# A flamingo-style stack of eight blocks: the second half of a mixture's gathers and additions moved into the attention behind it

## What is computed

```python
# layer 0, feed-forward (router on the normalised x)
topv, topi = jax.lax.top_k(probs, 2)
topv = topv / (topv.sum(axis=-1, keepdims=True) + 1e-09)
h = gelu(einsum('td,edh->teh', xf, w1)); y = einsum('teh,ehd->ted', h, w2)
out = einsum('te,ted->td', cw, y)
# layer 1, cross-attention (X: normalised x, C: context)
sim = sigmoid(sim_beta + sim_alpha * einsum('bkd,btd->bkt', C, X))
mask = one_hot(argmax(sim, axis=1), K, axis=1)
agg = einsum('bkt,btd->bkd', sim * mask, X) + C
out_k = agg / (sum(mask, axis=-1, keepdims=True) + 1.0)
out = X + einsum('bkt,bkd->btd', sim, out_k)
# in both cases
x = x + tanh(gate) * out
```

## Time and profile before

| what | value |
|---|---|
| median of 3 runs | 1840.54 us (1837.99 to 1843.1) |
| the profiled execution | 1836.82 us |
| its span, first to last instruction | 1835.1 us |
| granted PE clock over the span | 0.917 |
| PE, DVE, ACT, POOL busy | 1515.9, 1082.8, 683.5, 782.4 us |
| last experts' matmul to the attention's first instruction | 509 to 559.7 us |
| competitive attention | 559.7 to 642.9 us |

### The profile page before, as it was taken

The page is one execution under the profiler, slowest core; times in us unless marked ns, Lnnn a source line. Parts: engine busy times, 40 slices in busy tenths (PEclk is TensorE's granted clock), DMA queues, the critical chain, the costliest instruction groups (busy, mean ns, idle before and its releaser), DMA issues. The chain is left out here.

```text
span 1835.1 us, 32265 instructions
## 1 busy us (share of the span) xinstructions
PE 1515.9 (83%) x10543; PEld 1188.7 (65%) x10543; DVE 1082.8 (59%) x2434; ACT 683.5 (37%) x1673; POOL 782.4 (43%) x1037
## 2 busy tenths in 40 slices
PE   2998786799905786888887888789999999869997
PEld 1776675699904654666664444578778788658874
DVE  2666763323436978677775888455465765444555
ACT  2555443233304332344443333244454544411121
POOL 1444374513362444344443333145445377533335
PEclk9999897899955588899998999899999999969999
DMA  8000003477610000000000000000000000048853
GB/s 276 28 0 2 1 26 108 142 224 234 191 51 4 0 1 1 1 0 0 0 0 1 0 0 0 1 1 0 0 1 1 1 17 15 25 126 238 234 160 87
DMA packets 90876, 100.94 MB, mean 55 GB/s; under 512 B 11156, under 2 KB 73804, under 8 KB 90125
## 3 DMA queue, kind: packets, MB, share of 16 engines
q1 hardware_dynamic: 53490, 69.07, 12.2%
q0 software_dynamic: 8192, 16.79, 3.2%
q10 hardware_dynamic: 29083, 13.66, 2.6%
HBM read 70.92 MB, written 28.57 MB: 54 GB/s over the span
## 5 line engine op out<-in xcount | busy, mean ns | idle before, releaser
L427 POOL TENSOR_TENSOR exp_scores<-exp_scores,softmax_recip 128x308 f32<-128x308 f32 x256 | 181.7, 742 | 242.8 <-DVE softmax_recip L590 242.7
L916 POOL DMA_INDIRECT gathered_rows_ffn<-sorted_y,slot_ffn x128 | 121.0, 945 | 212.5 <-DMA sorted_y<-expert_rows_ffn 143.0
L612 PE MATMUL psum<-identity,exp_scores 128*77 128x128 f32 x1024 | 157.0, 290 | 41.1 <-POOL exp_scores L427 37.9
L1115 PE MATMUL psum<-sorted_transposed_ffn,tile_weights_ffn 128*128 128x256 f32 x736 | 184.2, 394 | 2.5 <-DVE sorted_transposed_ffn L1023 2.4
L612 PEld LDWEIGHTS psum<-identity,exp_scores 128*77 128x77 f32 x1024 | 119.6, 154 | 66.6 <-issue 32.6
L1773 POOL TENSOR_TENSOR exp_scores_xattn<-exp_scores_xattn,softmax_recip_xattn 128x1640 f32<-128x1640 f32 x32 | 93.5, 2921 | 160.8 <-DVE softmax_recip_xattn L1946 160.8
L442 ACT COPY probs_transposed<-psum 77x512 f32<-77x512 f32 x192 | 111.8, 584 | 131.8 <-PE psum L612 130.3
L1115 PEld LDWEIGHTS psum<-sorted_transposed_ffn,tile_weights_ffn 128*128 128x128 f32 x736 | 135.8, 195 | 27.6 <-DVE sorted_transposed_ffn L1023 12.2
L1124 PE MATMUL psum<-tile_weights_ffn,hidden_ffn 128*128 128x128 f32 x1104 | 138.5, 276 | 0.0
L700 PE MATMUL psum<-probs_transposed,v_padded 77*32 77x128 f32 x2048 | 128.9, 275 | 6.7 <-ACT probs_transposed L442 6.7
L1124 PEld LDWEIGHTS psum<-tile_weights_ffn,hidden_ffn 128*128 128x128 f32 x1104 | 131.0, 192 | 0.2
(11 more groups left out here) (358 smaller groups left out, 3402.8 us busy)
## 6 DMA issues: line engine op xcount, KB each, us to landing
tile_weights_ffn<-in_L_ffn_packed_dram SPq DMA_DIRECT2D x46, 512.0 KB, 3.5
tile_weights_ffn<-in_L_ffn_packed_dram SPq DMA_DIRECT2D x46, 384.0 KB, 3.4
sorted_rows_ffn<-sorted_x SPq DMA_DIRECT2D x92, 128.0 KB, 3.9
sorted_y<-expert_rows_ffn ACTq DMA_DIRECT2D x92, 128.0 KB, 3.3
sorted_x<-zeros SPq DMA_DIRECT2D x4, 1472.0 KB, 13.7
x_residual<-in_x_dram SPq DMA_DIRECT2D x4, 512.0 KB, 11.6
sorted_x<-xn_ffn,slot_ffn POOLq DMA_INDIRECT x128, 2.2
gathered_rows_ffn<-sorted_y,slot_ffn POOLq DMA_INDIRECT x128, 3.0
```

The costliest lines, as they stand in the source:

```text
L427: nc.gpsimd.tensor_tensor(e[:, par, heads, :], e[:, par, heads, :], rec.to_broadcast([S, HG, KC]), ALU.mult).then_inc(s["probs_ready"], 1)
L612: last = nc.tensor.transpose(m.psum[0:KC, 4 + g % 2, h * S:(h + 1) * S], e[:, nxt, g * HG + h, :], m.ident[:, :])
L916: nc.gpsimd.indirect_dma_start(yg[:, n % 4, k, :], None, m.sorted_y[half][:, :], bass.IndirectOffsetOnAxis(slot[:, half, k, b:b + 1], 0)). ...
L1115: mm = nc.tensor.matmul(m.psum[:, 2 * (n % 2) + half, c * TILE:(c + 1) * TILE], w[:, n % DEPTH, at:at + 128], xst[:, n % 2, :], start=True ...
```

## The change

The mixture of layer 0 is built with `tail=False`: POOL gathers nothing for the last 16 batches, and DVE's last loop of additions is gone. Both are now in the competitive attention, which takes the routing `r` (slots, weights and the gather buffers, that moved to it).

- POOL issues the gathers of four batches before step 0 and of three behind its own work of each of steps 0 to 3.
- DVE adds four batches at the end of step 0 and three at the end of each of steps 1 to 4, first all first rows, then all second rows, then the statistics.
- The attention's first variance, square root and reciprocal are of the first 16 batches. Those of batches 16 to 23 are taken between steps 2 and 3 and those of batches 24 to 31 between steps 4 and 5: DVE's five instructions at the end of a step, ACT's square root and the table of the exponential again at the start of the next, DVE's reciprocal and shift ahead of its next step.
- All ten steps are written out; the loop is gone (`looped=2`).

```diff
+        self.gathered = sb("gathered_rows", [S, 4, 2, D])
...
-                    for b in range(HBATCH):
+                    for b in range(HBATCH if tail or half < HALVES - 1 else 0):
...
-                else:
+                elif tail:
                     for n in range(B - HBATCH, B):
                         combine(n)
...
+    FIRST = 4
+    PER_STEP = 3
+    MIDDLE = B - HBATCH + HBATCH // 2
+    STATS = {2: (B - HBATCH, MIDDLE, 1), 4: (MIDDLE, B, 2)}
+
+    def late_of(g):
+
+        if g < 0:
+            return range(0, FIRST)
+        return range(min(FIRST + g * PER_STEP, HBATCH), min(FIRST + (g + 1) * PER_STEP, HBATCH))
...
+                def gather(g):
+                    for i in late_of(g):
+                        n = B - HBATCH + i
+                        wait(pool, s["late_combined"], i - 3)
+                        for k in range(2):
+                            nc.gpsimd.indirect_dma_start(r.gathered[:, n % 4, k, :], None, m.sorted_y[HALVES - 1][:, :],
+                                                         bass.IndirectOffsetOnAxis(r.slot[:, HALVES - 1, k, i:i + 1], 0)).then_inc(m.gathered[0][n % 4], 16)
...
                 def step(g, par, front, middle, back):
+                    if g < 0:
+                        gather(g)
                     if middle:
...
+                    if g >= 0:
+                        gather(g)
+
+                pipeline(pool, step, NGB, looped=2)
...
-                nc.scalar.activation(m.sd[:, :], m.var[:, :], ACT.Sqrt, bias=m.eps[:, 0:1]).then_inc(s["sd_ready"], 1)
+                first = slice(0, B - HBATCH)
+                nc.scalar.activation(m.sd[:, first], m.var[:, first], ACT.Sqrt, bias=m.eps[:, 0:1]).then_inc(s["sd_ready"], 1)
...
+                    if g - 1 in STATS:
+                        lo, hi, before = STATS[g - 1]
+                        act.wait_ge(s["var_ready"], before + 1)
+                        nc.scalar.activation(m.sd[:, lo:hi], m.var[:, lo:hi], ACT.Sqrt, bias=m.eps[:, 0:1]).then_inc(s["sd_ready"], 1)
+                        preload(nc, m, ACT.Exp)
+                        act.wait_ge(s["shift_ready"], before + 1)
...
-                variance_of_x(nc, m, dve, s["parts_ready"], s["var_ready"])
-                rstd_of_x(nc, m, dve, s["sd_ready"], s["rstd_ready"], s["shift_ready"])
+                variance_of_x(nc, m, dve, s["parts_ready"], s["var_ready"], 0, B - HBATCH)
+                rstd_of_x(nc, m, dve, s["sd_ready"], s["rstd_ready"], s["shift_ready"], 0, B - HBATCH)
...
+                def combine(g):
+                    late = late_of(g - 1)
+                    for i in late:
+                        n = B - HBATCH + i
+                        dve.wait_ge(m.gathered[0][n % 4], 32 * (n // 4 + 1))
+                        nc.vector.scalar_tensor_tensor(m.x[:, n, :], r.gathered[:, n % 4, 0, :], r.weight[:, HALVES - 1, 0, i:i + 1], m.x[:, n, :],
+                                                       ALU.mult, ALU.add).then_inc(s["late_first"], 1)
+                    for i in late:
+                        n = B - HBATCH + i
+                        dve.wait_ge(s["late_first"], i + 1)
+                        nc.vector.scalar_tensor_tensor(m.x[:, n, :], r.gathered[:, n % 4, 1, :], r.weight[:, HALVES - 1, 1, i:i + 1], m.x[:, n, :],
+                                                       ALU.mult, ALU.add).then_inc(s["late_combined"], 1)
+                    for i in late:
+                        n = B - HBATCH + i
+                        dve.wait_ge(s["late_combined"], i + 1)
+                        nc.vector.bn_stats(m.moments[:, n, :], m.x[:, n, :]).then_inc(s["late_moments"], 1)
...
+                    if g - 1 in STATS:
+                        lo, hi, before = STATS[g - 1]
+                        rstd_of_x(nc, m, dve, s["sd_ready"], s["rstd_ready"], s["shift_ready"], lo, hi, before)
...
-                pipeline(dve, step, NGB)
+                    if g >= 0:
+                        combine(g)
+                    if g in STATS:
+                        lo, hi, before = STATS[g]
+                        dve.wait_ge(s["late_moments"], hi - (B - HBATCH))
+                        variance_of_x(nc, m, dve, s["parts_ready"], s["var_ready"], lo, hi, before)
+
+                pipeline(dve, step, NGB, looped=2)
...
-                phase(sparse_experts, 0, r, m.router_t, a["L0_ffn_packed"], None)
-        if first_phase < 3 <= last_phase:
-            phase(competitive_attention)
+                phase(sparse_experts, 0, r, m.router_t, a["L0_ffn_packed"], None, tail=False)
+                phase(competitive_attention, r)
```

More of the change, by code:

```diff
@@ L62, in pipeline @@
     step(1, 1, True, True, True)
-    with eng.Fori(0, (looped - 2) // 2) as i:
-        step(i * 2 + 2, 0, True, True, True)
-        step(i * 2 + 3, 1, True, True, True)
+    if looped > 2:
+        with eng.Fori(0, (looped - 2) // 2) as i:
+            step(i * 2 + 2, 0, True, True, True)
+            step(i * 2 + 3, 1, True, True, True)
     for i in range(looped, n - 2):
@@ L812, in expert_of_tiles, with sparse_experts @@
     nc.vector.tensor_scalar(r.expert[:, half, :], r.work_row[:, :], float(E0 - 1), None, ALU.min).then_inc(known, 1)
-def sparse_experts(nc, m, sem, layer, r, router_t, packed, shared_weights, clear, out=None):
+def sparse_experts(nc, m, sem, layer, r, router_t, packed, shared_weights, clear, out=None, tail=True):
     hidden = F0 if layer == 0 else F3
@@ L847, in sparse_experts @@
         y = sb("expert_rows", [128, 2, TILE // 128, D])
-        yg = sb("gathered_rows", [S, 4, 2, D])
+        yg = r.gathered
         if shared:
@@ L1180, in chain, with competitive_attention @@
     return link
-def competitive_attention(nc, m, sem, clear):
+def competitive_attention(nc, m, sem, r, clear):
     names = ("parts_ready var_ready sd_ready rstd_ready shift_ready neg_ready ones_ready xn_ready xt_in_psum xt_ready "
-             "z_in_psum exp_ready one_added xn_used x_moved best_ready weighted_ready sim_ready pick_ready simt_in_psum simt_ready agg_in_psum y_done x_done mid_link back_link")
+             "z_in_psum exp_ready one_added xn_used x_moved best_ready weighted_ready sim_ready pick_ready simt_in_psum simt_ready agg_in_psum y_done x_done mid_link back_link late_first late_combined late_moments")
     s = {n: sem(f"{n}_1") for n in names.split()}
@@ L1230, in step @@
                         nc.gpsimd.tensor_tensor(xg, xg, gated[:, :], ALU.add).then_inc(s["x_moved"], 1)
-                pipeline(pool, step, NGB)
+                    if g >= 0:
+                        gather(g)
+                pipeline(pool, step, NGB, looped=2)
             @block.scalar
@@ L1267, in step @@
                         nc.scalar.activation(sv, sv, ACT.Identity, bias=m.one[:, 0:1]).then_inc(s["one_added"], 1)
-                pipeline(act, step, NGB)
+                pipeline(act, step, NGB, looped=2)
                 preload(nc, m, ACT.Sqrt)
@@ L1362, in step @@
                         mm.then_inc(s["y_done"], 1)
-                pipeline(pe, step, NGB)
+                pipeline(pe, step, NGB, looped=2)
 def dense_feed_forward(nc, m, sem, clear):
```

## The result

The changed kernel took 1817.07 us (median of four runs, 1816.69 to 1818.13); the kernel before took 1840.47 us beside it (1837.99 to 1843.1). The ratio is 0.9874, with a 95% interval of 0.9856 to 0.9891: 23.4 us faster, where the prediction said 1813, a gain of 25.2, and a range of 1804 to 1822. The profiled execution took 1817.31 us with a span of 1815.6.

A forecast was written before the change was run, and what follows sets the result against it. The tail was taken as bound by POOL's gathers, the attention's steps by DVE. -47.3 + 12.0 + 5.0 + 3.5 + 2.5 - 0.9 = -25.2 us gave 1811.6 or 1815.3, so 1813 us; range 1804 to 1822.

The forecast's parts named there:

- The tail removed: End of layer 0's mixture: without its last gathers and additions the attention starts at 512.4 us, not 559.7: -47.3 us.
- bad end: Barrier between mixture and attention: it keeps 5.6 us instead of falling to 0.6, so removing the tail gains only 42.3 us.
- rival 1: Barrier after the mixture keeps its 5.6 us, which belongs to the block's end: gain 20.2 us, 1818 us; chance 0.14.
- The additions: DVE in the attention: sixteen batches at 0.75 us each, +12.0 us; 16.5 us if each addition waited for the one before.
- POOL against DVE: Attention steps 0 to 2: POOL, late from gathers, runs its three tensor instructions against DVE's additions: +5.0 us, ends 0 and 8.
- Two statistics: Steps 2 and 4 of the attention: DVE's extra small instructions and its wait for ACT's square root, 1.75 us twice: +3.5 us.
- The output matmul late: After the two mid-attention square roots, normalisation and matmuls finish after DVE reaches addition L1319: +2.5 us, 0 at full clock.
- The covered wait: Before step 1's reciprocal in the attention: step 0's additions fill DVE's 0.94 us wait for ACT: -0.9 us.
- The base: Starting time for the whole kernel: 1813 us, the middle between 1811.6 from the profiled execution and 1815.3 from the median.
- Rival 2: Attention: additions slip between POOL's instructions and PE runs warm; gain 33 to 35 us, 1804 us; chance 0.08.
- rivals 3 and 4: Attention gathers slow: 1.6 us each makes POOL the bound, 1821 us, chance 0.07; from 2.7 us the kernel is slower, 0.04.
- Rival 5: Attention: gathers and additions wait for each other over the ring of four buffers; gain 13 us, 1825 us; chance 0.05.

## Why the prediction was right or wrong

- **The tail removed: right in kind, 4.6 us too large.** -47.3 was forecast, -42.7 measured, next to the bad end of -42.3. The failed step is "POOL's last indirect DMA of the mixture starts near 487 us, long before the barrier, so I take 0.6 us". It did start that early (491.29), but it isn't what counts. I had compared blocks by where their last indirect DMA stands. What counts is how many indirect DMAs there are to drain, and whether POOL comes early enough to cover that. The changed mixture has 64, its drain takes 5.3 us although POOL had issued nothing for over 20, and since POOL still waits for the last stored rows, nothing covers it. Counted from the mixture's start, the rows had landed after 207.4 us before the change (511.87 - 304.50) and the changed attention starts after 212.5: 5.1 us more, and not 0.6. The bad end and rival 1 came near this by luck: their 5.6 us were what a lead of 2.6 us had left of a drain of 7.8, for 96. The argument against rival 1, that the second layer's attention has only 0.5 us, is of a block in which POOL issues no indirect DMA and says nothing of this one.
- **The additions, 12.0 us: right.** 0.72 us a batch where nothing else is in the way, 11.5 in all. The serial end (16.5) was priced rightly by the batch (0.98), but the block gave half of it back.
- **POOL against DVE, 5.0 us: near in size, wrong in place.** The run without gathers puts POOL's lateness at 5.0, and the addition held up in step 0 makes it 6.0, within the ends of 0 and 8. The lateness was read rightly: POOL's first product starts 2.34 us after the reduction in step 0 and 2.66 in step 1, and 2.3 and 2.7 had been forecast. The failed part is "I take it that DVE gets one instruction in between two of POOL", by which the additions would pay in steps 0 to 2. Only one did, in step 0. In all three steps the last pick paid, held over two products, and step 4, taken for free, cost 1.3 (2.30 and 0.91 us for its two picks in place of 1.20 and 0.69). Only where POOL waits for a semaphore does DVE get in. The rule from the Trainium skill that the prediction cites ("SBUF — State Buffer", section "Who interferes with whom"), that the second to come blocks fully, agrees with where L1366 ends, 0.35 us behind POOL's second product in each of steps 0 to 2. That it was the second to come is shown for step 2 alone: in steps 0 and 1 its recorded start is the earlier one (534.37 against 534.67, 546.43 against 547.05).
- **Two statistics, 3.5 us: right.** 564.44 to 566.00 and 590.02 to 591.56, 3.1 us, of it 0.37 twice in waiting for the root.
- **The output matmul late, 2.5 us: right.** Two waits of 1.27 us, and with the load moved two of 0.34. ACT starts 1.42 us after the root, as in the earlier trace rows.
- **The covered wait, -0.9 us: right.** Step 1's reciprocal has no wait, where the earlier trace rows show 0.94.
- **The block's length** was forecast at 104 to 105 us and is 103.9; its first reduction comes 11.57 us after its start, and 11.7 was forecast.
- **The base.** Going halfway from the profiled execution's time to the median cost 2.3 us of accuracy. The profile was lucky in a stage that the change doesn't touch. By the median alone, with the measured stages, it is 1818.5. Errors offset one another, too: the tail's 4.6 and the base's 2.3 made the forecast too low, while the block was taken 1.3 us too long and the median came out 1.4 under what the stages give.
- **The rivals.** 1 came true: forecast 1818. It had 0.14, too little where 5.6 and 7.8 us stood in the trace and 0.6 was an inference. Rival 2 is refuted by L1366, rivals 3 and 4 by gathers that stay 1.25 to 1.44 us apart, and the one issued inside a reciprocal (541.07, the reciprocal from 540.88 to 542.93) took its 0.95. Rival 5 is refuted by the absence of any DVE wait on a landing. Two gathers did wait for the ring, 1.47 us in step 0 and 0.72 in step 3, both in POOL's time, as the prediction had it for the first.

## What to carry to other kernels

A wait at a barrier can have a part that belongs to how one engine ends its block, and it shows only as far as that engine's lead over the others doesn't cover it. Before you count it as saved, ask which engine arrives last after the change and how much it has to finish then, or keep the whole price. An engine's idle time isn't free for another one's work if the newcomer makes a third thing late: the gathers cost DVE nothing, but pushed POOL's products under DVE's longest unprotected instruction. And where one profile lies off the median, look for the stage in which it does before you take a middle.

## What the runs showed of the hardware

- The drain of POOL's DMA queue at a block's end took 5.3 us in a block with 64 indirect DMAs (DVE's wait fell from 7.67 to 2.36 us without it), though POOL had issued the last one over 20 us before. By the distances at other boundaries it took 2.6 us for 32 (2.97 from POOL's last instruction to the next block) and 7.8 for 96 (8.19 to 8.21). A lead of POOL of 6.5 us covered it for 32, with 0.3 us of wait left, and not for 96, with 1.73.
- POOL's products, queued back to back, hold a DVE instruction with two tiles from SBUF for two of them (3.01 us in place of 0.69), and run at 1.04 to 1.05 us themselves. Where they start on time, beside the first picks, they take 1.24 to 1.33. A gap of 0.07 us between two was enough for DVE to get in (1.70 us).
- A table load for a waiting activation ran 9 us ahead of it. It took 1.28 us, and so did the load back, behind which the next instruction followed after 0.02 us.
- The same kernel took 1843 us on one chip and 1921 on another. In the profiles compared, the two mixtures were 33 and 45 us longer on the slower one (DMA share 0.37 against 0.58 in one window), while the attention's start to its first reduction took 11.56 to 11.58 us in seven runs on both.
